# Local attention: six of eight heads of a step turned by DMA, the value product after the output or v projection, oT_low on GpSimd

## What is computed

```
xn = layernorm(x)
q, k, v = split(xn @ Wqkv + bqkv)               # 16 heads of 32
scores = q @ kwin.T / sqrt(512), masked to |distance| <= 128
attn = softmax(scores) @ vwin
out = x + (attn @ Wout + bout) + bitlinear_ffn(xn)
```

## Time and profile before

| | us |
|---|---|
| median of 3 runs | 2489.19 |
| lowest and highest | 2489.1 to 2490.74 |
| the profiled execution's own time | 2490.75 |
| its span | 2489.0 |
| PE busy | 2434.9 (98%) |
| DVE busy | 1604.7 (64%) |
| ACT busy | 1458.1 (59%) |
| POOL busy | 356.2 (14%) |
| DMA queue 1 | 59.6% of 16 engines |

### The profile page before, as it was taken

The page is one execution under the profiler, slowest core; times in us unless marked ns, Lnnn a source line. Parts: engine busy times, 40 slices in busy tenths (PEclk is TensorE's granted clock), DMA queues, the critical chain, the costliest instruction groups (busy, mean ns, idle before and its releaser), DMA issues.

```text
span 2489.0 us, 57251 instructions
## 1 busy us (share of the span) xinstructions
PE 2434.9 (98%) x20284; PEld 2002.2 (80%) x20284; DVE 1604.7 (64%) x4448; ACT 1458.1 (59%) x3744; POOL 356.2 (14%) x606
## 2 busy tenths in 40 slices
PE   6999999999999999989999999999999999999998
PEld 5788888888888888867888888888888888888886
DVE  5455555554545555336777777777777777777775
ACT  6333333333333333337777777777777777777775
POOL 2011111111111111021111111111111111111111
PEclk9999999999999999999999999999999999999999
DMA  5744433344444333324777777777777877777775
GB/s 171 208 114 114 113 109 107 107 113 118 118 118 118 105 109 108 99 68 124 198 200 197 197 197 204 203 202 198 199 197 199 204 198 203 203 200 197 198 191 148
DMA packets 650287, 396.69 MB, mean 159 GB/s; under 512 B 25760, under 2 KB 605344, under 8 KB 649552
## 3 DMA queue, kind: packets, MB, share of 16 engines
q1 hardware_dynamic: 649920, 393.58, 59.6%
q0 software_dynamic: 144, 0.17, 0.0%
HBM read 211.98 MB, written 181.67 MB: 158 GB/s over the span
## 4 chain that ended last, share of the span: by engine, by line
PE 51%; DMA 2%; ACT 1%; issue 1%; DVE 1%; SPq 0%; ACTq 0%; DVEq 0%
PE job_ps L1303 13%; PE job_ps L1312 8%; PE job_ps L1321 7%; PE pT_ps L1406 7%; PE job_ps L1447 7%; PE score_ps L1390 7%; DMA turned_blocks<-wqkv_raw 1%; DMA wqkv_raw<-turned_blocks 1%; PE pT_ps L1411 1%; ACT wqkv_raw L1095 1%; ACT pT L1105 0%; SPq L1006 0%; PE score_ps L1321 0%; DVE wqkv_raw L1196 0%; PE job_ps L1467 0%
## 5 line engine op out<-in xcount | busy, mean ns | idle before, releaser
L1095 ACT ACTIVATE wqkv_raw<-wqkv_raw,neg_max 128x384 f32<-128x384 f32 (+1 forms) x1024 | 619.7, 607 | 330.1 <-DVE neg_max L1179 330.0
L635 ACT ACTIVATE relu<-up_ps,fc_scale 128x512 f32<-128x512 f32 x256 | 176.1, 688 | 633.3 <-PE up_ps L745 633.3
L1179 DVE CUSTOM_DVE_ANT_0 wqkv_raw<-score_ps,mask 128x384 f32<-128x384 f32 (+1 forms) x1024 | 503.3, 547 | 5.0 <-PE score_ps L1390 3.0
L696 DVE SCALAR_TENSOR_TENSOR sq<-up_ps,relu 128x512 f32<-128x512 f32 x256 | 177.1, 692 | 492.8 <-ACT relu L635 491.6
L755 PE MATMUL down_ps<-proj_T,sq_hi 128*128 128x512 f32 x1024 | 404.4, 395 | 2.0 <-DVE sq_lo L679 1.9
L757 PE MATMUL down_ps<-proj_T,sq_lo 128*128 128x512 f32 x1024 | 404.7, 395 | 0.0
L741 PE MATMUL up_ps<-f_xT_hi,fc_T 128*128 128x512 f32 x1024 | 399.4, 390 | 2.2 <-PEq L136 2.2
L743 PE MATMUL up_ps<-f_xT_lo,fc_T 128*128 128x512 f32 x1024 | 399.5, 390 | 0.0
L1303 PE MATMUL job_ps<-xT_hi,wqkv_hi 128*128 128x256 f32 x1024 | 330.3, 323 | 0.1
L1196 DVE STREAM_TRANSPOSE wqkv_raw<-wqkv_raw 128x384 f32<-128x384 f32 (+1 forms) x508 | 276.0, 561 | 45.5 <-ACT wqkv_raw L1095 42.1
L1303 PE MATMUL job_ps<-xT_hi,wqkv_lo 128*128 128x256 f32 x1024 | 289.6, 283 | 0.0
(11 more groups left out here) (152 smaller groups left out, 4276.4 us busy)
## 6 DMA issues: line engine op xcount, KB each, us to landing
turned_blocks<-wqkv_raw SPq DMA_DIRECT2D x123, 768.0 KB, 4.9
wqkv_raw<-turned_blocks SPq DMA_DIRECT2D x492, 192.0 KB, 3.7
xT_hi<-xT SPq DMA_DIRECT2D x65, 256.0 KB, 4.8
xT_lo<-xT SPq DMA_DIRECT2D x65, 256.0 KB, 4.8
xT<-f_xT_hi SPq DMA_DIRECT2D x64, 256.0 KB, 2.9
xT<-f_xT_lo SPq DMA_DIRECT2D x64, 256.0 KB, 3.0
part_in<-in_L_attn_x SPq DMA_DIRECT2D x64, 256.0 KB, 5.2
partial<-f_y SPq DMA_DIRECT2D x64, 256.0 KB, 2.0
```

The lines of the kernel that those rows point to most:

```text
L696: nc.vector.scalar_tensor_tensor(sq[:, s % 2, :], up_ps[:, s % 2, :], 0.0, relu[:, s % 2, :], ALU.max, ALU.mult).then_inc(sq_done, 1)
L1095: nc.scalar.activation(probs[:, u, cols], probs[:, u, cols], ACT.Exp, bias=neg_max[:, u:u + 1], scale=-1.0, accum_out=prob_sum[:, u:u + 1] ...
L1179: nc.vector.tensor_tensor_reduce(out=probs[:, u, cols], in0=score_ps[:, h, cols], in1=mask[:, cols], scale=-SCORE_SCALE, scalar=3e38, op0= ...
```

## The change

In attention_stage:

- Two of the four heads of b = 1 (MOVED = 2) leave TensorE. VectorE turns them in blocks (turn_pair) into pair_blocks, SP sends them out in four transfers (move_pair_out) and in with one (move_pair_in), into pair_moved. TensorE turns only the other two (TURNED = 2), each with its widened sums, and ScalarE copies two, after the first and the third exp.
- run_a and run_b go in halves. run_b stands ahead of the value product. The slots change with it: 3t + 1 is run_b, 3t + 2 the value product. The value product takes b = 0 first, then b = 1.
- scale_oT(t - 2) and oT_high(t - 2) stand at the start of step t on their engines, ahead of the minima and the exps; oT_low goes to GpSimd, at the start of its step.
- SP: blocks in stand behind the loads and stores and behind the pair's four transfers out; the pair's transfer in is the last.
- The DRAM buffers and the tiles are laid out so that a piece of a transfer is longer: turned_blocks has the partition first (12 x 128 values in one piece going out, 3 x 128 coming in, where 128 were); xT_hi and xT_lo have the slot ahead of the four parts (512 values in one piece, where 128 were). The pair's pieces have 192 values.
- For the last step, TensorE turns the pair of b = 1 as well (turn_last_pair) and VectorE copies it.

In prepare_feed_forward the small product of v moves from unit 2 to unit 6 (V_AT), the four turns of the first x tile are spread from units 12 to 15 to units 12, 13, 17 and 19 (X_AT), their low parts to units 14, 15, 17 and 18 on VectorE (X_LOW_AT), and the first low-rank product comes two units later.

```
--- before.py
+++ after.py
-        X_AT = FB - DC
-        LOW_AT = FB + COLS
-        U_AT = LOW_AT + COLS
+        V_AT = 6
+        X_AT = (FB - 4, FB - 3, FB + 1, FB + 3)
+        X_LOW_AT = (FB - 2, FB - 1, FB + 1, FB + 2)
+        LOW_AT = FB + COLS + 2
+        U_AT = FB + 2 * COLS
...
 
-def attention_stage(nc, loaded, xT_dram, partial, turned_dram, out):
+def attention_stage(nc, loaded, xT_dram, partial, turned_dram, pair_dram, out):
 
...
-        pT_moved = wqkv_raw[:, 2, :].rearrange("p (w q h t) -> p w q h t", q=STRIPS, h=HC, t=DH)
-        pT = sb("pT", [P, HC, 4, P], F32)
+        pT_moved = wqkv_raw[:, 2, :].rearrange("p (q w h t) -> p q w h t", q=STRIPS, h=HC, t=DH)
+        pair_blocks = sb("pair_blocks", [P, STRIPS, 3, MOVED, DH], F32)
+        pair_moved = sb("pair_moved", [P, STRIPS, 3, MOVED, DH], F32)
+        pT = sb("pT", [P, TURNED, 4, P], F32)
...
@@ -921,17 +924,17 @@
             return 3 * t % 2
 
         def pv_bank(t):
-            return (3 * (t + 1) + 1) % 2
+            return (3 * (t + 1) + 2) % 2
 
         def b_bank(t):
-            return (3 * t + 2) % 2
+            return (3 * t + 1) % 2
 
         def job_release(n):
 
             t, k = divmod(n, 3)
             if k == 0:
                 return (qk_done, job_a(t) + 1) if job_a(t) is not None else None
-            if k == 1:
+            if k == 2:
                 return (oT_scaled, t) if 1 <= t <= STEPS else None
             b = job_b(t)
             if b is None:
...
-                moved = turned_dram[t % 2 * STRIPS:(t % 2 + 1) * STRIPS, :, :, :]
                 sp.wait_ge(blocks_turned, HC * (t + 1))
                 if first == 0:
-                    sp.dma_start(moved.rearrange("a w p x -> p (a w) x"),
-                                 blocks.rearrange("p a w h t -> p (a w) (h t)")).then_inc(blocks_out, 16)
+                    sp.dma_start(turned_dram[t % 2, :, :, :, :].rearrange("p a w x -> p (a w x)"),
+                                 blocks.rearrange("p a w h t -> p (a w h t)")).then_inc(blocks_out, 16)
                 else:
-                    for a in range(STRIPS):
-                        sp.dma_start(moved[a, first:3, :, :].rearrange("w p x -> p w x"),
-                                     blocks[:, a, first:3, :, :].rearrange("p w h t -> p w (h t)")).then_inc(blocks_out, 16)
+                    sp.dma_start(turned_dram[t % 2, :, :, first:3, :].rearrange("p a w x -> p a (w x)"),
+                                 blocks[:, :, first:3, :, :].rearrange("p a w h t -> p a (w h t)")).then_inc(blocks_out, 16)
 
             def move_blocks_in(t):
                 i, _ = where(t)
                 first = blocks_seen(i, 0).start
-                sp.wait_ge(blocks_out, 16 * transfers_out(t + 1))
+                sp.wait_ge(blocks_out, 16 * (t + 1))
                 if t >= 1:
                     sp.wait_ge(pv_done, t)
                 for a in range(STRIPS):
-                    moved = turned_dram[t % 2 * STRIPS + a, first:3, :, :].rearrange("w (q j) x -> j (w q) x", j=DH)
-                    sp.dma_start(pT_moved[a * DH:(a + 1) * DH, first:3, :, :, :].rearrange("j w q h t -> j (w q) (h t)"),
+                    moved = turned_dram[t % 2, :, a, first:3, :].rearrange("(q j) w x -> j q (w x)", j=DH)
+                    sp.dma_start(pT_moved[a * DH:(a + 1) * DH, :, first:3, :, :].rearrange("j q w h t -> j q (w h t)"),
                                  moved).then_inc(blocks_moved, 16)
+
+            def move_pair_out(t):
+                i, _ = where(t)
+                last = blocks_seen(i, 1).stop
+                sp.wait_ge(pair_turned, MOVED * (t + 1))
+                for q in range(STRIPS):
+                    sp.dma_start(pair_dram[t % 2, q, :, :, 0:last, :].rearrange("a j w x -> j a (w x)"),
+                                 pair_blocks[q * DH:(q + 1) * DH, :, 0:last, :, :].rearrange("j a w h t -> j a (w h t)")
+                                 ).then_inc(pair_out, 16)
+
+            def move_pair_in(t):
...
@@ -1020,7 +1039,6 @@
                 i, c = where(t)
                 if is_moved(t):
                     move_blocks_out(t)
-                    move_blocks_in(t)
                 if c == 0 and 1 <= i < NT - XR + 2:
                     load_x(i + XR - 2, 1)
                 if c == 1 and i + XR - 1 < NT:
@@ -1029,6 +1047,10 @@
                     store_y(i - 1, c - 2)
                     if i < NT:
                         load_part(i, c - 2)
+                if is_moved(t):
+                    move_pair_out(t)
+                    move_blocks_in(t)
+                    move_pair_in(t)
             for b in range(2):
                 sp.wait_ge(y_stored[b], 16 * NT)
...
+            def oT_low(t):
+                pool.wait_ge(oT_hi_done, t + 1)
+                nc.gpsimd.tensor_tensor(oT_lo[:, t % OR, :], oT[:, :], oT_hi[:, t % OR, :].bitcast(F32), ALU.subtract
+                                        ).then_inc(oT_done, 1)
+
             for u in range(2):
                 copy_keys(u)
             for t in range(STEPS + 3):
+                if 2 <= t <= STEPS + 1:
+                    oT_low(t - 2)
                 b = job_b(t)
                 if b and b[0] == "out":
...
-                last = 4 if h >= HC - 2 else seen.stop
-                act.wait_ge(turned, heads_turned(t) + h + 1)
+                act.wait_ge(turned, heads_turned(t) + h - MOVED + 1)
                 if t >= 1:
                     act.wait_ge(oT_scaled, t)
-                nc.scalar.copy(pT[:, h, seen.start:last, :].rearrange("p w t -> p (w t)"),
-                               pT_ps[:, h % 2, seen.start * P:last * P]).then_inc(pT_done, 1)
+                nc.scalar.copy(pT[:, h - MOVED, seen.start:4, :].rearrange("p w t -> p (w t)"),
+                               pT_ps[:, h % 2, seen.start * P:4 * P]).then_inc(pT_done, 1)
 
             def oT_high(t):
...
-                for h in range(HC // 2):
+                if 2 <= t <= STEPS + 1:
+                    oT_high(t - 2)
+                for h in range(HC):
                     if t < STEPS:
                         exp(t, 0, h)
-                    if 1 <= t <= STEPS:
-                        copy_pT(t - 1, h)
-                for h in range(HC // 2, HC):
-                    if t < STEPS:
-                        exp(t, 0, h)
-                for h in range(HC // 2, HC):
-                    if 1 <= t <= STEPS:
-                        copy_pT(t - 1, h)
+                    if h % 2 == 0 and 1 <= t <= STEPS:
+                        copy_pT(t - 1, MOVED + h // 2)
                 if job_a(t) is not None:
                     qk_high(job_a(t), A_NUMBER[t], a_bank(t))
                 for h in range(HC):
                     if t < STEPS:
                         exp(t, 1, h)
-                if 1 <= t <= STEPS:
-                    oT_high(t - 1)
...
-                    dve.wait_ge(turned, HC * t)
+                    dve.wait_ge(pair_turned, MOVED * t)
+                    dve.wait_ge(turned, TURNED * t)
                 for h in range(HC):
...
+            def turn_pair(t, h):
+                i, _ = where(t)
+                seen = blocks_seen(i, 1)
+                dve.wait_ge(exped, 8 * t + HC + h + 1)
+                if h == 0 and t >= 1:
+                    dve.wait_ge(pair_out, 16 * STRIPS * t)
+                nc.vector.transpose(pair_blocks[:, :, seen.start:seen.stop, h, :].rearrange("p a w t -> p w a t"),
+                                    probs[:, HC + h, seen.start * P:seen.stop * P].rearrange(
+                                        "p (w a t) -> p w a t", a=STRIPS, t=DH)).then_inc(pair_turned, 1)
+
             def copy_moved_pT(t, h):
...
                                         job_ps[:, pv_bank(t), 0:T].rearrange("p (b t) -> p b t", t=P),
-                                        pT[:, HC - 2:HC, 3, :], ALU.mult).then_inc(oT_scaled, 1)
-
-            def oT_low(t):
-                dve.wait_ge(oT_hi_done, t + 1)
-                nc.vector.tensor_tensor(oT_lo[:, t % OR, :], oT[:, :], oT_hi[:, t % OR, :].bitcast(F32), ALU.subtract
-                                        ).then_inc(oT_done, 1)
+                                        pT[:, 0:2, 3, :], ALU.mult).then_inc(oT_scaled, 1)
 
...
                     add_out(b[1], b[2], B_NUMBER[t - 1], b_bank(t - 1))
+                if 2 <= t <= STEPS + 1:
+                    scale_oT(t - 2)
                 if t < STEPS:
...
                     find_max(t, 1)
-                if 1 <= t <= STEPS:
-                    scale_oT(t - 1)
                 if t < STEPS and not is_moved(t):
                     for h in range(HC):
                         copy_moved_pT(t, h)
+                if t < STEPS and is_moved(t):
+                    for h in range(MOVED):
+                        turn_pair(t, h)
                 if t < STEPS:
                     inverse_sums(t, 1)
-                if 1 <= t <= STEPS:
-                    oT_low(t - 1)
+                if t < STEPS and not is_moved(t):
```

(41 more changed lines are left out.)

97 lines of the change are left out of this document (62 added, 35 removed).

## The result

| | before | after |
|---|---|---|
| time, median (range) | 2489.49 us (2489.1 to 2490.74) | 2451.58 us (2450.27 to 2456.06) |
| ratio | 1 | 0.9844, 95% interval 0.9832 to 0.9856 |
| span of the profiled execution | 2489.0 | 2448.5 |
| first minimum of step 0 at | 1122.81 | 1125.34 |
| mean of the 127 steps that follow | 10.571 | 10.194 |

The change is faster by 38 us, where 99 were forecast; the time lies 1.6 us above the range, and in the band of rival B (2428 to 2465). The budget of the two spans: the start is 2.5 us later, 127 steps are each 0.377 shorter (-47.9), the end is 5.0 longer, together -40.4 of the 40.5 that the spans differ. So the question is why a step takes 10.19 us and not 9.8.

A forecast was written before the change was run, and what follows sets the result against it. VectorE and ScalarE waiting for each other were taken as the bound, TensorE close behind. 125 steps falling from 10.6 to 9.8 us gain 100; with -3 and +1.5, 101 off 2489.2 gives 2388, taken as 2390, range 2360 to 2450.

The forecast's parts named there:

- rival B: At the value product: the pair's transfers come late, TensorE waits, steps of 10.1 to 10.4, 2428 to 2465 us; chance 0.23.
- Bound of before: Kernel before: VectorE and ScalarE waiting for each other set the 10.6 us step, TensorE close behind with about 0.2 slack.
- The loops of the new kernel: Attention step: VectorE and ScalarE's loop 9.39 without add_out, 9.99 with it, mean 9.69; TensorE 9.70.
- the 0.1 for two loops that push each other: Attention step: 0.1 us added for two equally long critical loops and thin covers, giving 9.8 us a step.
- exp to q_hi: ScalarE's link in the step: two 384-column copies fewer, 0.72 us together, shorten it from 4.09 to 3.37.
- The transposes fit under the exps: VectorE, behind the second four minima: two transposes, 1.18 us, end at 3.09, under the 3.14 until the last exp.
- The wait for k_lo at run_b: TensorE ahead of run_b: its 0.20 us wait for VectorE's k_lo goes, as the value product comes later.
- GpSimd's oT_low: Moved to GpSimd: takes some 0.73 us and costs nothing, since what queues behind it is needed microseconds later.
- The ways in: Queue SP: pair lands 16.2 to 19.9 us after the first minimum, 17.3 taken, reader at 18.1, so no wait.
- DMA bytes: DMA engines: 2.89 MB a step, up from 2.10, takes 8.9 us at 324 GB/s, so not the bound.
- Rival C: DMA engines become the bound at 256 GB/s: 11.3 us a step, 2577 us, slower; chance 0.08.
- Start and end: Preparation: -3 us (0 to -6) from moved work; last step: +1.5 us for two more heads turned on TensorE.

The follow-up runs named there:

- Experiment 7: The kernel before with only oT_low moved from VectorE to GpSimd: 2470.36 us, ratio 0.9941.
- Experiment 2: The changed kernel with only one of three key blocks of the pair's transfers moved, the four heads' whole: 2404.76 us, ratio 0.9664.
- experiment 5: The changed kernel with the old layouts, 512-byte pieces again for xT and the four heads: 2469.84 us, ratio 0.9933.
- experiment 4: The changed kernel with the preparation of the kernel before and, on GpSimd, bias additions ahead of oT_low: 2440.44 us, ratio 0.9816.
- experiment 1: The changed kernel with one of three key blocks of all moved heads going out and in, a third of the bytes: 2386.11 us, ratio 0.959.
- experiment 8: The changed kernel with the value product again ahead of the second projection or output product, the pair kept: 2678.14 us, ratio 1.0754.

## Why the prediction was wrong

**Where the 62 us went.** 52 of them lie in the steps (100 forecast, 48 measured), 5.5 at the start and 3.5 at the end.

**Bound of before: right for the steps with an add_out.** Experiment 7 moved only VectorE's work and won 19 us; a kernel bound by TensorE alone would have stayed.

**The loops of the new kernel: right.** 9.69 and 9.70 were forecast, 9.8 with the 0.1 for two loops that push each other, and 9.77 measured in the steady part with light transfers. The terms hold one by one: exp to q_hi 3.37 (1802.79 to 1806.16 in ScalarE's timeline), q_hi to second minimum 1.66 for 1.68, 3.14 to the reciprocal. The transposes fit under the exps with 0.20 left for the 0.05 of the forecast, since two took 1.03 and not 1.18. The wait for k_lo at run_b is gone. GpSimd's oT_low took 0.74, forecast 0.73. An add_out costs next to nothing in a step now, since TensorE ends last either way: with light transfers 9.80 with one and 9.74 without, where 9.99 and 9.39 were forecast for VectorE's loop.

**The ways in: the step that failed.** It has two halves, the pair's landing, which was taken too short, and the four heads' landing, which got no term at all. For the pair the sum was set out rightly, and the wrong end was taken: "I take landings nearer to the light ones, 17.3, because the pair is two sets of 384 KB and not 768 KB, and so no wait". Term by term, after the first minimum: turned 8.7 (SyncE issues at 8.6); last of four issued 10.1 (10.0); landed 12.1 to 15.0 (13.35); way in issued 12.5 to 15.0 (13.5); its landing 3.7 to 4.9 (4.9, the heavy end); so 18.4, where 17.3 was taken and the reader stands at 17.8. The mis-sized term is the last landing. A transfer of half the size landed no sooner than one of 768 KB had in the earlier trace rows, because it shares the DMA engines with the four heads' way in, issued 0.4 to 3.1 us into the step, and with the four heads' next way out, at 4.7. Experiment 2 shows the same: with a third of its bytes it still takes 4.2; with a third of all bytes 2.3.

The four heads' way in was put behind the pair's four transfers out, and the sum used that only to date the pair's issue. No term says where they themselves land. By the prediction's own rows a sum would have come out in time: issued at 10.1, 1.9 of issuing, landed after 3.7 to 4.9, so 15.7 to 16.9, with the reader at 17.45. Measured, the four are issued from 10.5 to 13.2, and the last lands at 17.35 in the median and up to 18.7, with the reader at 17.2. The issuing took 2.6 us and not 1.9. And 3.7 is a median over all four: in the kernel before the last of them already took 4.5 from its own issue. In time this half weighs as much as the other: 29 us of waits each.

**And a landing was taken for a number.** With the reader at 18.1 by my own sum, 17.3 left 0.8 us. Landings of one transfer spread from 4.1 to 6.4 us around 4.9, so steps are late even where the median is in time. Rival B had the place of the wait and the mechanism for the pair, not for the four heads; that the time falls into its band is in part luck, since 9 of the 62 us are the start and the end. The forecast should have put the pair's lateness at B's price with more than 0.23.

**DMA bytes: right about the bound, wrong in the rate.** 324 GB/s at a full share was taken; it is 286 / 0.95 = 301. The bytes of a step then take 9.7 us of the engines, not 8.9. Rival C (256) was further off. The share of 0.95 is inside the 0.85 to 0.95 that I listed, but only because the steps are longer; at 9.86 a step it is 0.99. The Trainium skill, DMA: Bandwidth & Descriptors, section Specifications, has line rate from 512 bytes on; by that the 512-byte pieces of experiment 5 should cost nothing. They cost 18 us and bring the full-share rate from 301 to 269 GB/s, far less than the 256 to 324 of the earlier trace rows that I had laid on them.

**Start and end: small, the start with the wrong sign.** -3 was forecast for the preparation, and the first minimum came 2.5 us later. The new preparation is slower (first up product at 59.42 against 56.24 before), but with the old one in experiment 4 the first minimum was as late, so what makes it late is open. For the last step +1.5 was forecast, and it was +5.0. In the change oT_low stands in GpSimd's queue ahead of the bias additions, so at the end the last two additions wait for it; in the kernel before they ended 10 us ahead of the end of the span. With the additions first, experiment 4 got 1.9 of the 5.0 back; the rest is open. GpSimd's timeline at the end of the changed kernel:

```profile
2442.00 0.72 POOL L1093 TENSOR_TENSOR oT_lo<-oT,oT_hi 128x256 fp32r<-128x256 f32 x1 [5.05 <-ACT oT_hi L1141]
2442.68 2.52 POOL L1088 TENSOR_TENSOR wout_raw<-wout_raw,out_bias 128x512 f32<-128x512 f32 x2
```

In the prediction oT_low's queue was looked at for a middle step only, where what stands behind it is needed microseconds later.

## What to carry to other kernels

A transfer's landing time belongs to what else is in flight as much as to its size: before a road through DRAM is called covered, add it up with the landings of the heaviest neighbours, and ask for a margin as wide as their spread (here 1.5 us), since each late one stretches its step and an early one gives nothing back. Where an issuing queue works in order, a step's transfers form one chain; splitting one in four costs the issue time of all that stand behind, so split on the side with nothing urgent behind it. When a new set of transfers goes into that queue, date the landing of every set behind it anew, also of those that didn't change: here half of the waits were the four heads', whose bytes hadn't changed. Undo the order and the parts singly before crediting any of them: here undoing the order costs 227 us, only because the pair is there, and some 100 of them are a granted clock that fell with the waits.

## What the runs showed of the hardware

- 384 KB as one transfer of 128 partitions landed in 4.1 us, as two of 64 partitions in 3.7 each, as four of 32 partitions in 2.8 each (medians). From the first issue to the last landing that is 4.1, 4.6 and 4.95 us: the parts are together slower than the whole.
- A transfer of 128 KB landed 2.3 us after its issue beside light neighbours (experiment 1) and after 4.2 beside the four heads' full ones (experiment 2).
- SyncE took 0.33 us to issue one transfer of 384 KB, 1.8 for four of 96 KB and 2.0 for six of 128 bytes (medians). The four heads' four took 2.6 in the change and 1.8 with a third of all bytes; single sets took up to 3.4 in both, so full DMA engines aren't the only thing that holds issuing up.
- The mean share of the DMA engines doesn't tell whether transfers are late: 0.95 with 10.19 us a step, 0.99 with 9.86, 0.86 with 9.83.
- With waits of up to 5 us at the value product the granted clock was 0.92 in experiment 8; in the change, with waits of up to 1.4, it was 1.00.
